# Exponentials and row maxima over two banks at a time in the attention of a fused transformer block

## The reference

```python
q = (x @ wq.T).reshape(B, S, 16, 16)              # 16 heads of 16
k = (x @ wk.T).reshape(B, S, 4, 16)               # 4 key heads, each for 4 query heads
v = (x @ wv.T).reshape(B, S, 4, 16)
k, v = jnp.repeat(k, 4, axis=2), jnp.repeat(v, 4, axis=2)
attn = jnp.einsum('bqhd,bkhd->bhqk', q, k) * scale
attn = jnp.where(causal, attn, -jnp.inf)
attn = softmax(attn, axis=-1)
out = jnp.einsum('bhqk,bkhd->bqhd', attn, v).reshape(B, S, C) @ wo.T
h = x + out
out = h + moe(rmsnorm(h))                         # two of 8 experts per token
```

## Time and profile before

| | |
|---|---|
| median of 3 runs | 2114.61 us (2113.46 to 2119.59) |
| profiled execution, its time | 2111.37 us |
| its span, first to last instruction | 2109.7 us |
| TensorE busy | 97% of the span |
| VectorE, ScalarE, GpSimd busy | 64%, 53%, 46% |
| 384 row maxima (L1248) | 250.0 us of VectorE, 681 ns each |
| 256 + 128 exponentials (L1139) | 138.5 + 66.1 us of ScalarE, 599 and 603 ns each |
| mean granted TensorE clock | 0.976 of full speed |

### The profile page before, as it was taken

How to read it: one execution, slowest core, us unless ns; L and a number is a source line. 1 busy time by engine, 2 the same in 40 slices (tenths; PEclk the granted TensorE clock), 3 DMA queues, 4 the chain that set the end, 5 groups by cost and what they waited for, 6 DMA issues and landing times. The chain is left out here.

```text
span 2109.7 us, 50236 instructions
## 1 busy us (share of the span) xinstructions
PE 2036.1 (97%) x17544; PEld 1752.2 (83%) x17544; DVE 1347.3 (64%) x2818; ACT 1117.4 (53%) x2219; POOL 963.0 (46%) x1062
## 2 busy tenths in 40 slices
PE   7999989999999999989979999999899999999997
PEld 7999985666666666659979999999888888888886
DVE  7888954676777767765636776788654444444452
ACT  6777744666666666655543333344354444454542
POOL 0000002365565556556644444444245656565653
PEclk9999987999999999989989999999999999999998
DMA  8767711133233232229864444544344444545442
GB/s 294 264 260 267 261 59 31 62 104 96 92 108 110 87 106 96 78 92 305 300 218 144 148 151 142 175 150 151 104 96 109 95 111 95 112 96 111 96 83 30
DMA packets 134682, 289.62 MB, mean 137 GB/s; under 512 B 23026, under 2 KB 64755, under 8 KB 128243
## 3 DMA queue, kind: packets, MB, share of 16 engines
q1 hardware_dynamic: 84466, 177.25, 24.9%
q0 software_dynamic: 50048, 110.14, 20.3%
HBM read 187.17 MB, written 95.42 MB: 134 GB/s over the span
## 5 line engine op out<-in xcount | busy, mean ns | idle before, releaser
L1248 DVE TENSOR_REDUCE neg_max<-ring 128x2 f32<-128x512 f32 (+1 forms) x384 | 250.0, 681 | 106.4 <-PE ring L1734 106.1
L1041 POOL TENSOR_SCALAR_AFFINE_SELECT weights_diag<-weights_diag 128x512 f32<-128x512 f32 x256 | 158.3, 643 | 258.4 <-ACT weights_diag L1139 258.1
L2908 POOL DMA_INDIRECT out<-q_t,row_put x128 | 201.8, 1576 | 162.4 <-ACT q_t L2972 137.7
L3046 DVE TENSOR_TENSOR ex_hid<-ex_up_ps,gelu 128x512 f32<-128x512 f32 x128 | 86.9, 688 | 171.8 <-ACT gelu L2956 171.8
L2956 ACT ACTIVATE gelu<-ex_gate_ps 128x512 f32<-128x512 f32 x128 | 76.3, 596 | 187.3 <-PE ex_up_ps L62 187.3
L2379 POOL DMA_INDIRECT picked_rows<-results,lo_row_now x128 | 134.0, 1047 | 56.3 <-issue 29.8
L1139 ACT ACTIVATE weights_diag<-ring 128x512 f32<-128x512 f32 x256 | 138.5, 599 | 24.2 <-PE ring L1752 24.2
L60 PE MATMUL ex_down_ps<-ex_dn_lo,ex_hid_hi 128*128 128x256 f32 x512 | 145.1, 283 | 2.8 <-issue 2.8
L61 PE MATMUL ex_down_ps<-ex_dn_hi,ex_hid_lo 128*128 128x256 f32 x512 | 145.2, 284 | 0.0
L62 PE MATMUL ex_down_ps<-ex_dn_hi,ex_hid_hi 128*128 128x256 f32 x512 | 144.9, 283 | 0.0
L1049 POOL DMA_INDIRECT sorted_rows<-h_sb,row_now x128 | 126.8, 990 | 34.8 <-issue 31.3
(11 more groups left out here) (404 smaller groups left out, 7521.8 us busy)
## 6 DMA issues: line engine op xcount, KB each, us to landing
ug_raw<-in_w_ug SPq DMA_DIRECT2D x32, 1028.0 KB, 5.0
dn_raw<-in_w_dn SPq DMA_DIRECT2D x32, 640.0 KB, 5.2
q_t<-sorted_rows SPq DMA_DIRECT2D x136, 128.0 KB
moe_w<-in_expert_gu SPq DMA_DIRECT2D x16, 1024.0 KB, 4.8
results<-c0n POOLq DMA_DIRECT2D x33, 256.0 KB, 4.4
x_raw<-in_x_t SPq DMA_DIRECT2D x32, 256.0 KB, 5.1
c0n<-c SPq DMA_DIRECT2D x32, 256.0 KB, 4.3
c0r<-c SPq DMA_DIRECT2D x32, 256.0 KB
```

What stands on the lines that cost most here:

```text
L1041: nc.gpsimd.affine_select(part, part, [[0, G], [1, P]], ALU.is_ge, 0.0, base=0, channel_multiplier=-1).then_inc(kept_done, 1)
L1248: nc.vector.tensor_reduce(out, src, AX_X, ALU.max, negate=True).then_inc(max_done, 1)
L2908: nc.gpsimd.indirect_dma_start(out=out_rows, out_offset=bass.IndirectOffsetOnAxis(ap=at, axis=0), in_=eo[c][:, n, :], in_offset=None, comp ...
L3046: nc.vector.tensor_tensor(hid[f % 2][:], up_ps[f % 2][:], gelu[f % 2][:], ALU.mult).then_inc(hid_done, 1)
```

## The change

The ring is allocated as three tensors of two adjacent banks instead of six of one, in the same places. `exps` and `maxima` take a half (groups 0 and 1, or 2 and 3) instead of a group and work on both banks in one instruction with 1024 columns, which adds 2 to the count when it is done. `exps` waits for both groups' scores, `maxima` for the later group's. On ScalarE the order stays. On VectorE the maxima of a round now stand in two places instead of up to four; in the second round of a batch both are ahead of `keep_kv`, and the first of them, now with group 1 in it, is ahead of `inverse_sums(i, 1)`, `mark_both` and `divide(i, 1)`. The waits of TensorE and GpSimd are not edited.

```diff
-        ring = [bank(f"ring{n}") for n in range(SLOTS)]
+        ring_pairs = [ctx.enter_context(nc.psum_tensor(f"ring{n}", [P, 2, 512], F32)) for n in range(SLOTS // 2)]
+        ring = [ring_pairs[n // 2][:, n % 2, :] for n in range(SLOTS)]
...
+        def slot_pair(round_, h):
+            return ring_pairs[(2 * round_ + h) % (SLOTS // 2)]
...
-            def exps(b, r, groups):
+            def exps(b, r, h):
                 tile = (weights_diag1[b[1] % 2], weights_diag0, weights_full)[r]
-                for g in groups:
-                    act.wait_ge(turned_done[g], times(3, b, r + 1))
-                    nc.scalar.activation(tile[:, g, :], slot(2 * r, g)[:], ACT.Exp).then_inc(exp_done, 1)
+                act.wait_ge(turned_done[2 * h], times(3, b, r + 1))
+                act.wait_ge(turned_done[2 * h + 1], times(3, b, r + 1))
+                nc.scalar.activation(tile[:, 2 * h:2 * h + 2, :], slot_pair(2 * r, h)[:], ACT.Exp).then_inc(exp_done, 2)
...
-            def maxima(b, r, g):
-                dve.wait_ge(scores_done, times(12, b, 4 * r + g + 1))
-                bank_ = slot(2 * r + 1, g)[:]
+            def maxima(b, r, h):
+                dve.wait_ge(scores_done, times(12, b, 4 * r + 2 * h + 2))
+                banks, groups = slot_pair(2 * r + 1, h)[:], slice(2 * h, 2 * h + 2)
...
-                nc.vector.tensor_reduce(out, src, AX_X, ALU.max, negate=True).then_inc(max_done, 1)
+                nc.vector.tensor_reduce(out, src, AX_X, ALU.max, negate=True).then_inc(max_done, 2)
...
                     maxima(s, 0, 0)
                 if picks:
                     mean_squares2(m_pick)
-                if has_scores:
-                    maxima(s, 0, 1)
                 if has_next:
                     front.norm_low(dve, i[1] + 2)
                 if has_scores:
-                    maxima(s, 0, 2)
-                    maxima(s, 0, 3)
+                    maxima(s, 0, 1)
...
                     maxima(s, 1, 1)
                 if has_next:
                     front.keep_kv(dve, i[1] + 2, k_t[(i[1] + 2) % 4], v[(i[1] + 2) % 4])
-                if has_scores:
-                    maxima(s, 1, 2)
-                    maxima(s, 1, 3)
...
                 if has_scores:
                     maxima(s, 2, 0)
-                    maxima(s, 2, 1)
...
                 if has_scores:
-                    maxima(s, 2, 2)
+                    maxima(s, 2, 1)
                 if picks:
                     scaled_odds(m_pick)
-                if has_scores:
-                    maxima(s, 2, 3)
```

More of the change, by code:

```diff
@@ L799, in attention_phase @@
         done_sb = [normed[:], c0n[0][:], c0n[1][:], weights_diag0[:, 0, :].rearrange("p (c d) -> p c d", c=2)]
-        turned = [ring[n][:].rearrange("p (c k s) -> p c k s", c=2, k=KT) for n in (2, 3, 4)]
-        product = [ring[n][:].rearrange("p (c d) -> p c d", c=2) for n in (5, 0, 1)]
+        turned = [ring[n].rearrange("p (c k s) -> p c k s", c=2, k=KT) for n in (2, 3, 4)]
+        product = [ring[n].rearrange("p (c d) -> p c d", c=2) for n in (5, 0, 1)]
         set_done = sem("at_set_done")
@@ L1164, in body @@
                 if has:
-                    exps(i, 0, (0, 1))
+                    exps(i, 0, 0)
                 if exists(later(i, 3)):
@@ L1168, in body @@
                 if has:
-                    exps(i, 0, (2, 3))
+                    exps(i, 0, 1)
                 if has_next:
@@ L1174, in body @@
                 if has:
-                    exps(i, 1, (0, 1))
+                    exps(i, 1, 0)
                 if has_h:
@@ L1178, in body @@
                 if has:
-                    exps(i, 1, (2, 3))
+                    exps(i, 1, 1)
                 if has_h:
@@ L1182, in body @@
                 if has:
-                    exps(i, 2, (0, 1))
+                    exps(i, 2, 0)
                 if has:
-                    exps(i, 2, (2, 3))
+                    exps(i, 2, 1)
                 if exists(later(i, 1)):
@@ L1240, in _ @@
         def _(dve):
-            def maxima(b, r, g):
-                dve.wait_ge(scores_done, times(12, b, 4 * r + g + 1))
-                bank_ = slot(2 * r + 1, g)[:]
+            def maxima(b, r, h):
+                dve.wait_ge(scores_done, times(12, b, 4 * r + 2 * h + 2))
+                banks, groups = slot_pair(2 * r + 1, h)[:], slice(2 * h, 2 * h + 2)
                 if r < 2:
-                    out, src = neg_max[1][:, g, 2 * r:2 * r + 2], bank_.rearrange("p (j s) -> p j s", j=2)
+                    out, src = neg_max[1][:, groups, 2 * r:2 * r + 2], banks.rearrange("p g (j s) -> p g j s", j=2)
                 else:
-                    out, src = neg_max[0][:, g, :], bank_.rearrange("p (j s) -> p j s", j=G)
-                nc.vector.tensor_reduce(out, src, AX_X, ALU.max, negate=True).then_inc(max_done, 1)
+                    out, src = neg_max[0][:, groups, :], banks.rearrange("p g (j s) -> p g j s", j=G)
+                nc.vector.tensor_reduce(out, src, AX_X, ALU.max, negate=True).then_inc(max_done, 2)
             def keep_shift(i):
@@ L1732, in scores @@
                         rows = slice(32 * g, 32 * g + 32)
-                        out = slot(2 * r + 1, g)[:].rearrange("p (c s) -> p c s", s=keys)[:, :, q * P + 32 * n:(q + 1) * P]
+                        out = slot(2 * r + 1, g).rearrange("p (c s) -> p c s", s=keys)[:, :, q * P + 32 * n:(q + 1) * P]
                         last = nc.tensor.matmul(out, at.placeb[rows, n, :], at.maskb[rows, 0:len(heads_), 0:left_], start=False, stop=(n == NKV - 1))
@@ L1751, in turned_scores @@
                     rows = slice(32 * g, 32 * g + HD + 1)
-                    nc.tensor.matmul(slot(2 * r, g)[:], k_t[n][rows, k * P:(k + 1) * P], q_t[n][rows, :, q * P:(q + 1) * P],
+                    nc.tensor.matmul(slot(2 * r, g), k_t[n][rows, k * P:(k + 1) * P], q_t[n][rows, :, q * P:(q + 1) * P],
                                      start=True, stop=True).then_inc(turned_done[g], 1)
```

## The result

| | before | after |
|---|---|---|
| median of 13 runs | 2115.47 us | 2124.77 us |
| ratio, 95% interval | | 1.0043 [1.0033, 1.0052] |
| span of the profiled execution | 2109.7 us | 2121.1 us |
| VectorE busy | 64% | 63% |
| `neg_max` reductions | 384, 250.0 us | 192, 233.3 us |

The edit does what it says: 16.7 us of VectorE and 12.3 us of ScalarE are gone. The kernel is 9.3 us slower all the same, by the medians, and 11.4 us by the spans. The forecast was 2115.4 with a range up to 2123, and 77% of the chance on "no difference".

The account below looks back on a forecast made before the run. TensorE was taken as the bound (548.0 of 550 us busy in the steady part), so VectorE and ScalarE savings counted as 0. Terms -1.5 + 2.6 + 0 - 0.3 = +0.8 us gave 2115.4 us, range 2111 to 2123.

Parts of the forecast that it names:

- the wait for both banks: Start of each merged instruction: 0 to 0.05 us later than the first of its pair, taken as 0.01.
- step 4: Ends of the attention phase: waits at loop start 0.05 to 0.07 us shorter each, last batches 0; -0.3 us in all.
- Step 1: Round 1 scores on TensorE, awaiting the merged exponential: 0.05 us gained in each of 29 batches, -1.5 us.
- Step 2, odd batch: Query projection behind the division, which the reordered maxima delay 0.53 us: slack of 0.58 shrinks to 0.05, no stall.
- Step 2, even batch: Query projection: later GpSimd masks hold `chosen`, delaying the division; stall 0.14 to 0.27, taken as 0.20, x 13, +2.6 us.
- Step 3: Keeping keys and values behind the second merged maximum, awaited by the gate's matmuls: even batch a tie, 0; odd 0.
- the hold at its bound with 0.05 more for both banks everywhere: Rival: `chosen` hold of 0.35 in all 13 batches, 0.05 more wait in every batch; +5.0, 2119.6 us; chance 0.2.
- the price of the instructions: Slower rival: two-bank instructions save nothing, each at its upper bound; +12 us, 2127; chance 0.12.

Follow-up runs that it names:

- f: Kernel before, each pair of exponentials waiting for both groups' scores but still run as two instructions; 5.7 us over before by the medians.
- l: Kernel before with only round 0's exponentials merged; odd steps 19.31 us, even steps 19.75 us (before 19.32 and 19.52).
- h: Changed kernel with `chosen` ahead of the merged maximum of groups 0 and 1 of round 1; 4% slower.
- c: Kernel before with only the row maxima merged, in the changed order, exponentials one bank at a time; 6.8 us over before by the medians.
- m: Changed kernel with `chosen` behind the division of query tile 1 instead of ahead of it; 2123 us, even step 19.73 us.
- g: Changed kernel with a one-column exponential that loads Exp's table before the first scores are awaited; loop's first step 23.2 us (26.3 in after), time did not fall.
- i: Changed kernel with round 1's exponentials and maxima one by one in their old places and the Exp table loaded early; median 10 us over before.
- a: Changed kernel with one semaphore count per half, so each merged exponential waits once instead of twice; odd step 0.02 us shorter.
- k: Kernel before with only round 2's exponentials and the maxima of rounds 0 and 2 merged; ratio 1.0004 [0.9994, 1.0015].
- n: Kernel before with `chosen` behind the division of query tile 1; no change, steps forecast at 19.52 and 19.32 us, time at 2115.
- b: Kernel before with only the exponentials merged, two waits each, row maxima as before; 6.5 us over before by the medians.
- d: Changed kernel with one wait per merged exponential and round 1's merged maxima behind query tile 1's division; odd steps 19.36 us, even 19.96.

## Why the prediction was wrong, step by step

Two steps of the prediction failed: the wait for both banks, which turns the steady loop from a forecast +1.1 us into +5.0, and step 4, the ends of the phase, which is the larger by size, +5.8 instead of -0.3.

**Waiting for both banks (failed; the term was mis-sized).** Predicted 0 to 0.05 us, taken as 0.01; f measures 0.11 for the exponentials, and the odd batch 0.10 for the maxima (0.19 instead of 0.09 behind the block). The prediction had no row for when a pair's second bank is complete, and took the side-by-side groups for simultaneous. The bound was set by that belief instead of by a row.

**Step 1.** Predicted -0.05 us a batch; the block went from 1.53 to 1.61 (+0.08). The merged exponential is 0.06 shorter than the pair but starts 0.11 later, and group 2 waits for all of it. The sign was wrong through the step above.

**Step 2, odd batch.** Predicted no stall, with 0.05 of the slack of 0.58 left. The 0.52 came as priced; the wait for both banks came on top twice, 0.07 us in round 1's block and 0.10 at the reduction, where 0.06 of slack were left: queries at 597.05 - 588.82 = 8.23 instead of 8.11. By the next block of scores it is 9.14 (597.96) instead of 8.96 (590.77); the first of the query matmuls takes 0.39 us where it took 0.33, and the later ones follow 0.06 later. The odd step is +0.17.

**Step 2, even batch.** Right, mechanism and size. Predicted: masks 0.30 to 0.43 later, `chosen` held to their end, queries 0.14 to 0.27 late, taken as 0.20. Measured: 0.35, held, 0.19. l shows the cause by itself. The prediction had `chosen` held by the last mask alone; h shows it held by the whole run of masks, which here comes to the same. One slip: the sum let step 1's gain of 0.05 count in these batches too, where the hold would have swallowed it, as it swallowed c's loss.

**Step 3.** Called a tie, and it is one (m): keys and values end just when the delayed TensorE comes.

**Step 4, the ends (failed; effects put at nothing).** Predicted -0.3 us, measured +5.8 in the profiles (start +3.9 net, first picking step +1.1, last +0.8). Three things were missing. The table load moved behind the wait, 1.3 us (g). It does so wherever round 0's exponentials wait for both banks (but in g and i, which load early): in f, which merges nothing, and in a, which has one wait. In their traces the wait ends at the load, where before it ended at the exponential. In the first picking step, second, GpSimd's queue has no scatter behind the masks but an addition, and `chosen` is held to its end:

```profile
418.87 1.15 DVE L1321 TENSOR_TENSOR chosen<-one_hot 128x32 bf16<-128x32 f32 x1
...
418.70 1.26 POOL L1058 TENSOR_TENSOR x_sb<-x_sb,h_sb 128x512 f32<-128x512 f32 x1
...
420.40 0.39 PE L60 MATMUL piece_a<-nt_lo,wqk_hi 128*128 128x256 f32 x1 [0.83 <-DVE o L1268]
```

Before, `chosen` ran from 413.90 to 414.49, begun ahead of the addition (414.40). Third, the last batches were called filled, and in the last step TensorE waits 0.51 us for VectorE; k, with merged maxima and single exponentials in round 0, shows the same. And some 0.9 us of the start is this one profile of before, whose third step ended at 368.3 us, while those of k and n, as fast, ended at 369.2. The remaining 1 to 2 us go with the clock, which is only argued: from 312 to 324 us it is granted at 0.50 (all at 1.2 GHz) in after and in m, and at 0.64 in before and all other kernels. What decides that is open.

**The rivals.** The one nearest to the result, "the hold at its bound with 0.05 more for both banks everywhere", gave 2119.6; it has both places of the steady loop, none of those at the ends, and half the size. The prediction put the slow end on the price of the instructions, which was known to a hundredth, instead of on the wait, which was not known at all. The Trainium skill (Perfetto Trace Analysis, section Optimizing Scalar/DVE Operations) advises to break up instructions that hold up another engine; the awaited instructions here bear this out at 0.10 us a step for each engine.

## What to carry to other kernels

An instruction over two banks waits for the later bank and releases the earlier one late. Merge it where nobody waits (k: no change in the steady loop, 0.9 us in the last step), not where another engine stands behind it (f, l: +0.10 and +0.23 us a step), and expect no gain from it while TensorE is the bound. Count what depends on the *start* and on the *first half* of each instruction, on every engine down to the masks, and look where a table load ends up when the wait in front of its instruction changes. A bound for an unknown wait must come from a row: here a belief of "a few hundredths" stood for 0.11 us. So must a term put at nothing: here the ends of the phase, at -0.3 us, cost 5.8. Together they turned a forecast of no change into a miss.

## What was not expected of the hardware

**Short stalls and the clock.** In this loop TensorE runs at 2.4 GHz without a break. Stalls of 0.8 us (a and c, first picking step) were followed by half the clock and a step 5.6 us longer, while the same stall in after was not; stalls of 1.38 us (h) by 10 to 13 us at half clock nearly every time. In b, d, g, i and l an even step that had grown by 0.2 to 0.4 us was sometimes 3.1 us longer still. In l, the step from 760.8 us has the same starts as its neighbours to 0.04 us, until the clock falls:

```profile
766.00:772.00 6.00, 5.96 (x75) 4.80 (x68) 5.44 (x12) 2.68 (x8) 5.50 (x8) 1.00 0.23 85
772.00:778.00 6.00, 6.00 (x66) 4.50 (x68) 1.36 (x5) 2.85 (x8) 0.44 (x1) 0.53 0.09 24
```

Before, k and n, whose even steps are 19.52 us, show none, nor do the single profiles of after, f and m. That a late even step is what opens the door to it fits all of these, but it was only argued. It could be part of why kernels with equal steps differ by several us in their medians.

**The hold.** `chosen` lasts 0.13 us in c, 0.28 in after, 0.62 before, 0.97 in i and l and 2.02 in h, with the same operands; in l, after and h it ends 0.04 to 0.05 us after GpSimd's last mask of the run. It was not released between two masks (h, from 0.4 us into the first to the end of the fourth). Yet in k's last step `own_rows`, begun at 892.96, is through at 893.61, with the masks running to 894.70. Nor did `chosen` always wait for what follows: in the first picking step before, it ended at 414.49, though GpSimd went from its masks (to 414.44) straight to the addition at 414.40. Whether an operation already begun is let through at such a change isn't settled.
